# Splitting the tokens in their natural layout and turning them by transposing transfers

## The reference

```python
h = relu(layernorm(x))                       # over the last axis, eps 1e-5
q, k, v = h @ Wq.T, h @ Wk.T, h @ Wv.T       # 16 heads of 32 columns
a = q k^T * 512 ** -0.5 + 2 * adj            # per head, 256 x 256
a = -inf in rows of a that are all zero
p = softmax(a), nan -> 0
out = x + (p v, heads side by side) @ Wo.T
```

## Time and profile before

| | |
|---|---|
| median of the runs | 1256.42 us |
| profiled execution: device time, span | 1256.68 us, 1254.9 us |
| PE busy | 1228.8 us, 98% of the span |
| PE weight loads busy | 1108.5 us, 88% |
| DVE, ACT, POOL busy | 1068.1, 1044.8, 898.7 us (85%, 83%, 72%) |
| granted TensorE clock | 1.000 of full speed |
| DMA | 163.89 MB, queue 1 at 50.3% of 16 engines |
| PE's transposes of h (L345) | 256 instructions, 40.2 us busy |

### The profile page before, as it was taken

One profiled execution on the slowest core, in us unless ns is written; L12 is line 12 of the kernel. 1 busy time (PEld: TensorE's weight loads), 2 busy tenths in 40 slices (PEclk: granted clock), 3 DMA queues, 4 the chain that ended last, 5 costly groups with the idle time before them and its releaser, 6 DMA issues.

```text
span 1254.9 us, 43727 instructions
## 1 busy us (share of the span) xinstructions
PE 1228.8 (98%) x13104; PEld 1108.5 (88%) x13104; DVE 1068.1 (85%) x3500; ACT 1044.8 (83%) x2427; POOL 898.7 (72%) x1266
## 2 busy tenths in 40 slices
PE   6899999999999999999999999999999999999997
PEld 5788989989989989889889899899999899898996
DVE  6788888888888888888888888888888888888887
ACT  5888888888888888888888888888888888888886
POOL 4767777777776777777777776777767777767765
PEclk9999999999999999999999999999999999999999
DMA  7355445465445464454564454654454554545533
GB/s 241 90 125 151 117 111 141 116 159 137 122 109 138 130 150 132 121 124 124 144 150 117 112 141 116 158 139 120 109 138 129 150 133 118 126 125 142 134 98 88
DMA packets 90773, 163.89 MB, mean 131 GB/s; under 512 B 14976, under 2 KB 23168, under 8 KB 90752
## 3 DMA queue, kind: packets, MB, share of 16 engines
q1 hardware_dynamic: 90752, 163.64, 50.3%
HBM read 46.14 MB, written 16.78 MB: 50 GB/s over the span
## 4 chain that ended last, share of the span: by engine, by line
PE 83%; issue 5%; DVE 5%; POOL 4%; ACT 3%; DMA 0%; DVEq 0%; ACTq 0%; POOLq 0%
PE job_ps L330 48%; PE pT_ps L405 15%; PE s_ps L394 8%; PE o_ps L426 5%; PE job_ps L345 2%; PE o_ps L427 2%; POOL fold L1006 2%; PE job_ps L370 2%; DVE minus L801 1%; ACT pT_hi L627 1%; DVE stats L694 1%; DVE pT_lo L810 1%; ACT probs L616 1%; ACT y L597 1%; POOL bounds L1012 0%
## 5 line engine op out<-in xcount | busy, mean ns | idle before, releaser
L1006 POOL TENSOR_TENSOR fold<-minus 128x512 f32<-128x512 f32 x256 | 326.7, 1276 | 245.2 <-DVE bounds L801 245.0
L616 ACT ACTIVATE probs<-minus,bounds 128x256 f32<-128x256 f32 x1024 | 461.6, 503 | 9.2 <-DVE bounds L801 9.1
L810 DVE TENSOR_TENSOR pT_lo<-pT_ps,pT_hi 128x512 f16<-128x512 f32 x512 | 350.7, 685 | 122.6 <-ACT pT_hi L627 122.2
L801 DVE CUSTOM_DVE_ANT_0 minus<-s_ps,adj_now 128x256 f32<-128x256 f32 x1024 | 389.3, 418 | 12.7 <-issue 6.1
L627 ACT ACTIVATE pT_hi<-pT_ps 128x512 f16<-128x512 f32 x512 | 305.9, 597 | 107.9 <-PE pT_ps L405 106.3
L405 PE MATMUL pT_ps<-ident,probs 128*128 128x128 f32 x2048 | 307.5, 273 | 1.7 <-ACT probs L616 1.6
L330 PE MATMUL job_ps<-hT_hi,w_hi 128*128 128x256 f16 x1024 | 280.2, 274 | 1.6 <-DVE hT_lo L762 1.2
L330 PE MATMUL job_ps<-hT_hi,w_lo 128*128 128x256 f16 x1024 | 278.9, 272 | 0.0
L330 PE MATMUL job_ps<-hT_lo,w_hi 128*128 128x256 f16 x1024 | 278.8, 272 | 0.0
L405 PEld LDWEIGHTS pT_ps<-ident,probs 128*128 128x128 f32 x2048 | 241.9, 140 | 19.0 <-ACT probs L616 2.3
L394 PE MATMUL s_ps<-qk_stack 96*128 96x256 f32 x1024 | 246.7, 323 | 2.1 <-DVE w_lo L748 1.2
(11 more groups left out here) (88 smaller groups left out, 2190.4 us busy)
## 6 DMA issues: line engine op xcount, KB each, us to landing
qk_stack<-qk_parts SPq DMA_DIRECT2D x768, 128.0 KB, 2.3
x_in<-x SPq DMA_DIRECT2D x32, 512.0 KB, 4.9
x_res<-x SPq DMA_DIRECT2D x32, 512.0 KB, 3.8
out<-y SPq DMA_DIRECT2D x64, 256.0 KB, 2.1
adj_in<-adj SPq DMA_DIRECT2D x32, 256.0 KB, 4.8
w_in<-wq SPq DMA_DIRECT2D x2, 512.0 KB, 6.0
w_in<-wk SPq DMA_DIRECT2D x2, 512.0 KB, 7.6
w_in<-wv SPq DMA_DIRECT2D x2, 512.0 KB, 9.6
```

What stands on the lines that cost most here:

```text
L616: end = nc.scalar.activation(probs[hh % 2][:, t, :], minus[hh // 2 % 2][:, hh % 2, t, :], ACT.Exp, bias=bounds[:, hh // 2 % 4, 2 * (hh % 2 ...
L801: end = nc.vector.tensor_tensor_reduce(out=minus[pair % 2][:, hh % 2, t, :], in0=s_ps[SCORE_BANK[hh]][:, t * N:(t + 1) * N], in1=adj_now[: ...
L810: nc.vector.tensor_tensor(pT_lo[hh % 4][:, :, :], pT_ps[hh % 2][:, :].rearrange("p (m n) -> p m n", m=NT), pT_hi[hh % 4][:, :, :], ALU.sub ...
L1006: nc.gpsimd.tensor_tensor(f1[:, :, :], src[:, :, 0:N // 2], src[:, :, N // 2:N], ALU.add).then_inc(folded1, 1)
```

## The change

- PE no longer transposes h, except in batch 0. The `h` jobs are gone from `JOBS`, so the banks of the remaining jobs are numbered anew (y 0 now follows v 3 in its bank).
- From batch 1 on ACT splits in the natural layout: `split_tokens` reads h and writes the high parts of both tiles to `h_parts` (one instruction, 128x1024, in head 9, for batch b + 2). DVE's `low_tokens` writes the low parts, tile 0 in head 11 and tile 1 in head 15.
- SP's `turn_tokens` then turns each tile by one transposing transfer of 128x1024 float16 into `hT[odd]`, of which there are two, for odd and even batches. Loops of PE and SP take two batches to a turn, since a batch's buffer stands in the code.
- The statistics of x move on DVE from heads 7 and 11 to heads 3 and 6, `normalise` on POOL from head 12 to head 7.
- Batch 0: the first weight halves are split by quarters (`first_split`), q and k are stacked by halves (`first_stack`, with `late_stacked`), v 0 goes to a bank of the transposed probabilities, some jobs swap banks, the first jobs stand in another order, Wo is split in quarters in heads 6 to 13.

The core of the diff (batch 0's reordering is cut):

```diff
-    4: [("h", 0, 1, 0, 4), ("y", 0, -1, 0, 6)],
-    5: [("y", 0, -1, 6, 9), ("h", 1, 1, 0, 4), ("y", 0, -1, 9, 12)],
+    4: [("y", 0, -1, 0, 6)],
+    5: [("y", 0, -1, 6, 12)],
...
-        hT_hi = sb("hT_hi", [P, KT, N], F16)
-        hT_lo = sb("hT_lo", [P, KT, N], F16)
+        h_parts = sb("h_parts", [P, NT, 2, D], F16)
+        hT = [sb(f"hT{i}", [P, NT, 2 * KT, P], F16) for i in range(2)]
...
+            def turn_tokens(b, t, odd, first):
+
+                sp.wait_ge(h_split, (b - 1) * NT + (t + 1))
+                settled(sp, "sp")
+                if not first:
+
+                    sp.wait_ge(ended["qk"], count("qk", 0, b - 1))
+                    settled(sp, "sp")
+                sp.dma_start_transpose(hT[odd][:, t, :, :], h_parts[:, t, :, :].rearrange("p a d -> p (a d)")
+                                       ).then_inc(h_turned[t], 16)
...
             sp.dma_start(x_res[:, :, :], x_d[0]).then_inc(res_loaded, 16)
-            load_tokens(1)
-            stack(0, 0, True)
+            for n in range(2):
+                first_stack(n)
+            for t in range(NT):
+                turn_tokens(1, t, 1, True)
...
                 if not last:
                     stack(0, b + 1, False)
+                if not ends:
+                    turn_tokens(b + 2, 0, odd, False)
                 if not first:
                     store(b - 1, 1)
 
                     sp.dma_start(x_res[:, :, :], x_d[b]).then_inc(res_loaded, 16)
+                if not ends:
+                    turn_tokens(b + 2, 1, odd, False)
...
-                            end = product(ps[:, i * N:(i + 1) * N],
+                            end = product(ps[:, i * N:(i + 1) * N].rearrange("p (t n) -> p t n", t=NT),
                                           [lambda k, w=m: w[:, k, n * P:(n + 1) * P] for m in (w_hi[w], w_lo[w])],
-                                          [lambda k, v=v: v[:, k, :] for v in hT], start - i * half, stop - i * half)
+                                          [lambda k, a=a: tokens[:, :, a * KT + k, :] for a in range(2)],
+                                          start - i * half, stop - i * half)
...
-            with pe.Fori(1, B - 1) as b:
-                body(b, False, False)
-            body(B - 1, False, True)
+            with pe.Fori(1, B - 1, 2) as b:
+                body(b, 1, False, False)
+                body(b + 1, 0, False, False)
+            body(B - 1, 1, False, True)
...
+            def split_tokens(b, first):
+
+                act.wait_ge(h_ready, b + 1)
+                if not first:
+
+                    for turned in h_turned:
+                        act.wait_ge(turned, (b - 1) * 16)
+                nc.scalar.activation(h_parts[:, :, 0, :], h[:, :, :], ACT.Relu).then_inc(h_high, 1)
...
+                    if first and hh == 0:
+                        split_tokens(1, True)
+                    if not (nearly or last) and hh == 9:
+                        split_tokens(b + 2, False)
...
+            def low_tokens(b, t):
+
+                dve.wait_ge(h_high, b)
+                nc.vector.scalar_tensor_tensor(h_parts[:, t, 1, :], h[:, t, :], 0.0, h_parts[:, t, 0, :],
+                                               ALU.max, ALU.subtract).then_inc(h_split, 1)
...
-                        if hh == 7:
+                        if hh == 3:
                             tokens_stats(b + 2, range(0, 1))
-                        if hh == 11:
+                        if hh == 6:
                             tokens_stats(b + 2, range(1, NT))
                             moments_of(b + 2, 2 * (b + 2))
+                        if hh in (11, 15):
+                            low_tokens(b + 2, (hh - 11) // 4)
+                    if first and hh in (1, 2):
+                        low_tokens(1, hh - 1)
...
-                    if not (nearly or last) and hh == 12:
+                    if not (nearly or last) and hh == 7:
                         normalise(b + 2, False)
```

More of the change, by code:

```diff
@@ L215, in weight_waits @@
         def weight_waits(engine, i, half):
-            engine.wait_ge(w_split, TURNS.index((i, half)) + 1)
+            engine.wait_ge(w_split, TURNS.index((i, half)) - 1)
         def bank(kind, n, b):
-            if isinstance(b, int) and (kind, n, b) == ("h", 1, 0):
+            if kind == "h":
+                return 1 - n
+            if isinstance(b, int) and (kind, n, b) == ("y", 1, B - 1):
                 return 1 - BANK[kind, n]
+            if isinstance(b, int) and (kind, n, b) in OTHER_BANK:
+                return 1 - BANK[kind, n]
+            if isinstance(b, int) and (kind, n, b) == ("v", 0, 0):
+                return 3
             return BANK[kind, n]
@@ L271, in _, with body @@
             sp.dma_start(x_res[:, :, :], x_d[0]).then_inc(res_loaded, 16)
-            load_tokens(1)
-            stack(0, 0, True)
-            def body(b, first, last):
+            for n in range(2):
+                first_stack(n)
+            for t in range(NT):
+                turn_tokens(1, t, 1, True)
+            def body(b, odd, first, last):
+                ends = last or isinstance(b, int) and b + 2 == B
                 if not (last or isinstance(b, int) and b + 2 == B):
@@ L515, in last_product @@
                     pe.wait_ge(last_taken, 2)
-                end = product(job_ps[BANK["y", n]][:, :], [lambda k, v=v: v[:, k, n * P:(n + 1) * P] for v in oT],
+                end = product(job_ps[bank("y", n, B - 1)][:, :], [lambda k, v=v: v[:, k, n * P:(n + 1) * P] for v in oT],
                               [lambda k, w=w: w[:, k, :] for w in (wo_hi, wo_lo)], start, stop)
@@ L643, in _, with body @@
             sum_weight(WQ, 1)
-            sum_weight(WV, 0)
             act.wait_ge(q_scales, 1)
             take("qk", 0, 0, True)
+            sum_weight(WV, 0)
             sum_weight(WV, 1)
             take("qk", 1, 0, True)
-            for i, half in TURNS[2:]:
-                high_weight(i, half)
+            high_weight(WQ, 1)
+            high_weight(WK, 1)
+            high_weight(WV, 0)
             copy_adj(0)
+            high_weight(WV, 1)
             exponentials(0, 0, True)
-            take("v", 0, 0, True)
             act.wait_ge(q_scales, 2)
             take("qk", 2, 0, True)
-            def body(b, first, last):
+            take("v", 0, 0, True)
+            def body(b, first, nearly, last):
                 for hh in range(HEADS):
@@ L850, in _ @@
             take("qk", 0, 0)
+            tokens_stats(1, range(NT))
+            moments_of(1, 2)
             weight_scales(WV, 0)
@@ L855, in _ @@
             query_scales(1)
-            for i, half in TURNS[2:]:
-                low_weight(i, half)
+            low_weight(WQ, 1)
+            low_weight(WK, 1)
+            low_weight(WV, 0)
             shift(0, 0, True)
+            low_weight(WV, 1)
+            shift(0, 1, True)
+            take("qk", 2, 0)
             take("v", 0, 0)
-            shift(0, 1, True)
-            tokens_stats(1, range(NT))
-            moments_of(1, 2)
-            take("qk", 2, 0)
             def body(b, first, nearly, last):
```

162 lines of the change are left out of this document (103 added, 59 removed).

## The result

The changed kernel takes 1329.0 us (median of 4 runs, 1320.2 to 1333.6), against 1256.8 us for the kernel before on the same chip: a ratio of 1.056 (95% interval 1.054 to 1.059), 5.6% slower. The forecast was 1260.5, with a range of 1230 to 1286. The time lies outside the range.

The account below looks back on a forecast made before the run. PE, busy 98% of the span, was taken to bound the kernel. To 1256.7 us came 29 x 0.17 = +4.9 for batches 1 to 29, -1.1 for batch 30 and 0 for the start: 1260.5, range 1230 to 1286.

Parts of the forecast that it names:

- What goes from PE: Heads 4 and 5: the transposes of h leave PE's loop, -0.53 and -0.44, together -0.97 us a batch.
- Head 4: Moved statistics delay DVE's take of v 3, PE's first y product waits: head 4 gives 0.13 us, not 0.53.
- The wait for h and the chain behind it: Heads 9 to 14: ACT's split waits 1.3 us for GpSimd's h, DVE turns late, v 0 starts 0.72 us late.
- DVE's low part of h: New DVE operation with two SBUF inputs, taken at 0.65 us, between 0.42 and 1.35.
- Rival 3: DVE's low part of h collides with GpSimd's fold: up to 0.8 us a batch, +23, 1284; chance 0.10.
- Rival 4: PE's two-batch loop is fetched anew on 14 returns, up to 4.9 us each: up to +69, 1329; chance 0.08.
- The transposing transfers: SyncE's queue: 1.5 us to issue one; x still lands 1.7 us ahead of its statistics, so hidden.
- Rival 2: Slow transposing transfers make x late, holding the statistics and PE in 29 batches: up to +133, 1394; chance 0.07.
- The start: Start and batch 0: most of 4.0 us saved, against 3 to 4 us waiting behind transposes; 0 net, bounds -4 and +3.
- Batch 30: The batch with neither statistics nor split: -0.97 - 0.18 = -1.1 us.

Follow-up runs that it names:

- flat_v2: As flat, split in head 10, tile 0 statistics in head 5, low parts in next head 0, transposing transfers before the stack, batch 0's x and adj first: 1221.7 us.
- flat_stats: As flat, with DVE's statistics of tile 0 behind the low part of the probabilities of head 4 instead of head 3: 1271.3 us, ratio 1.011.
- loop_split: The changed kernel with its PE loop of two batches, and only ACT's split moved from head 9 to head 10: 1288.5 us, ratio 1.023.
- loop_v2: As flat_v2, with PE's loop of two batches to a turn put back: 1255.6 us, ratio 0.999 to the kernel before.
- flat_low: As flat, with DVE's low parts of h in heads 0 and 4 of the next batch, second transposing transfer behind the stack: 1358.0 us, ratio 1.081.
- flat: The changed kernel with PE's batches 1 to 30 written out one after the other, no loop on PE: 1280.4 us, ratio 1.018.
- before_pe2: The kernel before, with only PE's loop changed to two batches a turn (14 returns): 1290.6 us, ratio 1.026.
- before_pe5: The kernel before, with only PE's loop changed to five batches a turn (5 returns): 1269.3 us, ratio 1.008.

## Why the prediction was wrong, point by point

- **What goes from PE, -0.97 a batch.** Right. flat_v2, where PE waits for nothing in a steady batch, has it in full, and 0.2 more.
- **Head 4.** Right: 0.4 to 0.48 of wait where 0.4 was forecast, for the take of v 3; flat_stats takes it away.
- **The wait for h and the chain behind it.** Mechanism right, size off. Forecast +0.72, 0.4 of it at head 12; measured +0.33 at head 12 and +0.90 at head 14. The term mis-sized is DVE's low part of h, taken at 0.65 "because width sets the time on DVE in every row". It was 1.28 in its place. Rival 3 had the collision, priced at up to 0.8 a batch with a chance of 0.10. With head 4 and head 5 the batch comes to +0.69 against the forecast +0.17: 15 of the 77 us.
- **The return of PE's loop.** This is the step that failed. The prediction's sum has no term for it: "Batches 1 to 29 have the whole pattern: 29 x 0.17 = +4.9". Rival 4 had the mechanism, its sign in q8 and a bound (4.9 a return, 1329), with a chance of 0.08. It cost 56 of the 77 us: 4.0 a return, 2.3 to 2.4 for the gap and the rest for the clock behind it, which rival 4 didn't have. That the bound meets the time measured, 1329, is chance: the returns cost 56 where it took 69, and 21 us came from elsewhere. That the trace before showed no fetching was no evidence: it showed a body of 860 instructions that stays, and the body had doubled. The body of some 1680 was fetched anew at each return, although it is below the room that rival 4 names.
- **The transposing transfers.** Right in the steady batch: 1.28 to issue (1.5 taken), 4.5 to land, and neither x nor the operand was waited for. Rival 2 didn't occur. The estimated 10.5 us worked out from the Trainium skill's page "VectorE: DVE Perf Modes", section "The three transpose paths", did not show, nor did the estimated 1.0 from its page "DMA: Bandwidth & Descriptors", section "Latency and other measured facts"; the landing, 3.1 to 6.5 us, lies between them.
- **The start.** The mechanism named against it, the transposes ahead of x and the stack, is what happened: DVE 3.4, PE 5.4. It turned 4.0 won by head 0 into a net +2.1, inside the bounds of -4 and +3. flat_v2's order of the queue gives -3.6.
- **Batch 30.** -1.1 forecast, -0.9 measured.

Open: why the load of q8 starts only 0.5 us ahead of the gap in the changed kernel and 1.0 in the others (loop_split, which takes only ACT's stall away, has 1.0), and what brings the clock down behind some gaps and not behind others.

## What to carry to other kernels

When an edit needs two buffers and therefore a loop over two iterations, count the instructions of the longest engine's body first: here PE's doubled body cost 2.0 to 2.4 us at each return, and some 1.8 more where the clock fell, which took nearly all that the edits won (33.9 of 36.8 us in loop_v2) or more than that (in the changed kernel), while the same program written out cost nothing, and five iterations to a turn 12 us in all. An operation moved to new operands has to be priced beside what runs next to it: DVE reading two SBUF operands under POOL's fold took nearly twice its time (1.23 instead of 0.68 us). And a transfer that is put into an in-order queue is judged by what is behind it and by the head that first reads it: with the second transposing transfer behind the stack, flat_low took 78 us more than flat.

## What was not expected of the hardware

- PE's body of 860 instructions was not fetched anew in its loop; bodies of 1680 to 1730 and some 4300 cost a fetch at each return, 2.4 to 2.6 us by the medians of before_pe2, loop_v2 and before_pe5, whatever the length. Queue q8 moved 2.29 MB for 14 returns, 1.95 for 5, and 1.75 for the written-out program.
- Behind 13 of the 14 gaps of 2.0 to 2.6 us in the changed kernel PE's clock fell (0.58 over 4 us in the row above), which costs 1.6 to 1.8 us. Behind gaps of 1.5 to 2.1 it fell in 1 of 14 (before_pe2), 2 of 5 (before_pe5), 3 of 14 (loop_v2) and 4 of 14 (loop_split), the shortest of them 1.73, and behind one of 3.35 in flat_low it held.
- One transposing transfer of 128x1024 float16 takes SyncE 1.28 us to issue and lands 3.1 to 6.5 us later (median 4.5).
